# Expert feed-forward in blocks of 32 rows on four column quarters, with two rooms in DRAM for the sums

## The chip, the cores and the metric

The kernel runs on one core of a Trainium2 chip. The metric is device time in microseconds, the median of several executions. TensorE (PE) has a granted clock of 1.2 or 2.4 GHz; VectorE is DVE, ScalarE is ACT, GpSimd is POOL and SyncE is SP, which issues most DMAs.

## What is computed

Eight sequences of 100 tokens (800 in all), width 1024, go through two blocks. Block 0 is a cross attention with 16 heads over 722 context vectors and a mixture of experts; block 1 is another cross attention and a feed-forward with ternary weights. The change touches only the mixture of experts, 32 experts of inner width 512, four for each token:

```python
logits = x @ gate_w.T + gate_b
topk_logits, topk_idx = jax.lax.top_k(logits, K)              # K = 4, E = 32
topk_weight = jax.nn.softmax(topk_logits, axis=-1)
...                                                           # tokens sorted by expert
gate = jax.lax.ragged_dot(xt, w_gate, group_sizes) + b_gate[gid]
up = jax.lax.ragged_dot(xt, w_up, group_sizes) + b_up[gid]
gate = jnp.minimum(gate, 7.0)
up = jnp.clip(up, -7.0, 7.0)
activated = (up + 1.0) * gate * jax.nn.sigmoid(1.702 * gate)
outs = jax.lax.ragged_dot(activated, w_down, group_sizes) + b_down[gid]
...                                                           # back in the tokens' order
y = jnp.sum(outs * topk_weight[..., None], axis=1)
```

Everything is in fp32 here. An fp32 matmul of the program shows as two records in the trace.

## The kernel before

All engines run hand-written streams and meet at semaphores. The expert stage runs from `route_vector` (line 1557) to the sums added to X (lines 1933, 2071).

**Routing.** `route_vector` finds each token's four experts, counts tokens per expert, gives every expert whole blocks of BS rows (64 = P // G with G = 2) and puts a third of the blocks, in a row, on each of NQ_W = 3 queues (`rounds` blocks each): step s works on queue s % 3. An expert that lies across two queues is loaded twice, so there are 34 loads, three of them before the loop. It writes the lists of token indices per tile of 128 rows (`idx`), and the tables `need_b`, `need_d`: how many loads must have landed before step s. `slot_gates` (line 1710) does the gates and the target rows `sidx`, which the steps' columns come from.

**Steps.** `iterations` (line 1867) writes IT = 12 steps out once, and then a loop whose body is again 12 steps, in four guarded rounds of three. In step s the engines do this:

- PE (`moe_tensor`, line 1935; one step from line 1995): wait for weights part A (`m_wga`); first half of gate/up; transposes of the next tile's tokens (`turn`, line 1943, four of the tile's eight) and of the previous step's activations (`turn_act`, line 1959, two); second half of gate/up (part B); the down product of the previous step (line 1975). A block's 64 rows are 64 columns of the array: column half g computes outputs g x 512 to g x 512 + 511 of the gate and up weights, and the two halves work side by side on the same tokens. The down product is split over its 1024 outputs in the same way. So gate/up is 16 matmuls, down 8, each with a moving side of 512.
- DVE (`moe_vector`, line 2039): bias (line 2050), limits, product, into `act`.
- ACT (`moe_scalar`, line 2097): copies the transposes out of PSUM, the sigmoid, and `store` (line 2116): the down result times the row's gate into `ysb`, of which there are two.
- POOL (`moe_pool`, line 1880): gathers each tile's token rows from DRAM (line 1887), and scatters `ysb` with an adding DMA into `acc_d` in DRAM (line 1900), 128 rows of 512 values. Each scatter waits until the one before has landed (`m_sc`), since two blocks may hold the same token. `store` waits for the scatter two steps back.
- SP (`moe_sync`, from line 1780): one round of its loop for each further expert. Its weights come in three parts, A and B (gate/up) and D (down), 2 MB each, into one of three rooms `W2[:, q]`. A and B go out (line 1838) when the last gate/up of the room's former expert is done, the biases when its last `act` is, and D when its last down is.

**The end.** After the last scatter, `m_fin` lets SP load the sums (`yl`, seven tiles, line 1865); DVE adds four to X (line 2071), POOL three (line 1933). In between PE computes the down biases (line 2034). Then the second attention begins; its first loads are in `first_loads` (line 653).

## Time and profile before

| | us |
|---|---|
| median of 3 runs | 3527.59 (3527.23 to 3527.94) |
| the profiled run, its own time | 3528.64 |
| its span | 3526.9 |
| mixture's steps, from DVE's first read of gate/up in step 1 to that in step 68 | 1268.8 to 2041.4 |

The span is the stretch from the first to the last instruction in the profile, and the granted clock is near full throughout. Busy shares are of the whole span. Tables of groups give, for a line and an engine, busy time and mean duration of one, then the idle time of that engine just before these instructions and what ended it. A mean of PE is the duration of a pipelined record, which overlaps its neighbours; the pace is read from starts. In a timeline consecutive instructions of one line are merged.

### The profile page before, as it was taken

What the parts mean: (1) busy time and instruction counts of PE and PEld (TensorE: products, weight loads), DVE (VectorE), ACT (ScalarE), POOL (GpSimd) and SP (SyncE); (2) the same over time, 40 slices, a digit from 0 to 9 for tenths busy, and PEclk for the clock granted to TensorE, in tenths of its full rate; (3) what the DMA queues carried; (4) which work ended last, traced back from release to release, by engine and by line L of the source; (5) the groups of instructions that cost most, each with busy time, mean ns of one, the idle gap of its engine ahead of it and who ended that gap; (6) DMA issues with size and microseconds to landing.
All of it is one profiled execution on the core that took longest, in us unless ns stands there. A gap on an engine that the chain in (4) does not pass through costs nothing.

```text
span 3526.9 us, 43045 instructions
## 1 busy us (share of the span) xinstructions
PE 3433.0 (97%) x16460; PEld 1800.5 (51%) x16461; DVE 1634.7 (46%) x1977; ACT 863.2 (24%) x1256; POOL 746.3 (21%) x709
## 2 busy tenths in 40 slices
PE   7999999999999789999999989999999999999999
PEld 4565565566466333333333346556465564554554
DVE  8764474565466531111111146436355365662661
ACT  2330131032033211111111125335154252220110
POOL 4200400400320012212222220000000002780860
PEclk9999999999999899999999999999999999999999
DMA  7631131132123196899888975436255261430420
GB/s 219 227 101 52 62 88 47 67 100 64 49 69 123 67 376 198 303 380 313 292 294 308 369 240 163 138 126 184 95 166 157 80 163 57 144 142 1 158 93 38
DMA packets 93029, 556.64 MB, mean 158 GB/s; under 512 B 11288, under 2 KB 11424, under 8 KB 74976
## 3 DMA queue, kind: packets, MB, share of 16 engines
q1 hardware_dynamic: 58288, 445.28, 35.5%
q0 software_dynamic: 31392, 93.76, 10.3%
q10 hardware_dynamic: 3216, 15.68, 1.4%
q8 instruction: 101, 1.65, 0.2%
q14 instruction: 32, 0.26, 0.0%
HBM read 517.62 MB, written 40.71 MB: 158 GB/s over the span
## 4 chain that ended last, share of the span: by engine, by line
PE 85%; DMA 6%; DVE 3%; ACT 1%; issue 1%; SPq 0%; POOL 0%; DVEq 0%; POOLq 0%; ACTq 0%
PE PS L964 15%; PE PS L1951 10%; PE PS L2276 10%; PE PS L1111 9%; PE PS L921 8%; PE PS L1975 5%; DMA W<-in_W 5%; PE PS L2302 5%; PE PS L950 4%; PE PS L816 4%; PE PS L833 3%; PE PS L900 2%; PE PS L1047 2%; PE PS L848 2%; PE PS L974 1%; ACT Sb L1250 1%
## 5 line engine op out<-in xcount | busy, mean ns | idle before, releaser
L964 PE MATMUL PS<-Sb,kvN 121*128 121x400 f32 (+1 forms) x1536 | 536.7, 499 | 0.0
L1951 PE MATMUL PS<-W,hT 128*64 128x512 f32 x2208 | 505.1, 599 | 14.8 <-DMA W<-in_W 14.4
L964 PEld LDWEIGHTS PS<-Sb,kvN 121*128 121x128 f32 (+1 forms) x1536 | 286.7, 190 | 205.9 <-issue 2.4
L2276 PE MATMUL PS<-xh,wq 128*128 128x400 f16 x2048 | 348.8, 334 | 1.8 <-DVE xh L1339 1.8
L2050 DVE TENSOR_TENSOR gu<-PS,bias 128x512 f32<-128x512 f32 x69 | 47.7, 691 | 634.4 <-PE PS L1951 607.0
L921 PE MATMUL PS<-kvT,wkr 128*128 128x363 f32 x1024 | 340.4, 475 | 0.0
L1111 PE MATMUL PS<-wb,ctxl 128*128 128x512 f32 x768 | 331.0, 592 | 0.0
L2232 POOL TENSOR_SCALAR gtq<-stg,thr 128x1024 f16<-128x1024 f32 x96 | 289.1, 3026 | 170.2 <-DMA stg<-in_F 142.5
L1951 PEld LDWEIGHTS PS<-W,hT 128*64 128x64 f32 x2208 | 155.5, 138 | 303.4 <-issue 292.8
L1515 POOL TENSOR_TENSOR qrope<-qrope,rt 128x400 f32<-128x400 f32 x156 | 157.5, 1034 | 719.0 <-DVE rt L1377 712.7
L2276 PEld LDWEIGHTS PS<-xh,wq 128*128 128x128 f16 x2048 | 200.8, 98 | 149.2 <-DVE xh L1339 2.3
L1975 PE MATMUL PS<-W,actT 128*64 128x512 f32 x1104 | 250.5, 596 | 2.6 <-ACT actT L2105 2.6
L1111 PEld LDWEIGHTS PS<-wb,ctxl 128*128 128x128 f32 x768 | 145.8, 190 | 181.9 <-issue 179.9
L921 PEld LDWEIGHTS PS<-kvT,wkr 128*128 128x128 f32 x1024 | 185.1, 190 | 100.6 <-issue 2.6
L1422 DVE TENSOR_TENSOR Sb<-Sb,PS 121x2400 f32<-121x2400 f32 x64 | 169.9, 2654 | 91.9 <-PE PS L1033 91.9
L1476 DVE TENSOR_TENSOR X<-PS,X 128x512 f32<-128x512 f32 x96 | 66.3, 691 | 277.0 <-PE PS L1111 277.0
L1163 ACT ACTIVATE KR<-PS 128x726 f32<-128x726 f32 x128 | 99.3, 776 | 375.7 <-PE PS L921 375.7
L816 PE MATMUL PS<-xnT,wq_h 128*128 128x400 f32 x512 | 185.8, 500 | 1.7 <-ACT xnT L515 1.7
L950 PEld LDWEIGHTS PS<-QR,KR 64*121 64x121 f32 x3072 | 168.2, 182 | 33.8 <-issue 32.2
L1438 DVE RECIPROCAL rz<-PS 128x400 f32<-128x400 f32 x64 | 169.5, 2649 | 24.4 <-PE PS L974 24.4
L950 PE MATMUL PS<-QR,KR 64*121 64x100 f32 x3072 | 179.7, 270 | 0.0
L2302 PE MATMUL PS<-wdq,hh 128*128 128x512 f16 x768 | 166.6, 379 | 0.0
(287 smaller groups left out, 3781.3 us busy)
## 6 DMA issues: line engine op xcount, KB each, us to landing
W<-in_W SPq DMA_DIRECT2D x96, 2048.0 KB, 10.7
stg<-in_F SPq DMA_DIRECT2D x32, 1536.0 KB, 6.4
kvT<-kvT_d SPq DMA_DIRECT2D x64, 726.0 KB, 4.3
kvN<-kvN_d SPq DMA_DIRECT2D x64, 726.0 KB
absin<-in_F POOLq DMA_DIRECT2D x48, 512.0 KB, 4.0
hn<-in_F POOLq DMA_DIRECT2D x48, 512.0 KB, 4.7
wb<-in_WB SPq DMA_DIRECT2D x8, 2560.0 KB, 9.5
wc_h<-in_WC SPq DMA_DIRECT2D x32, 576.0 KB, 4.6
```

The costliest lines, as they stand in the source:

```text
L816: mm = nc.tensor.matmul(PS[:, heads_bank(a, half, first), 0:HALF], wq_h[a % 2][:, c * K:(c + 1) * K], xnT[:, c, half * HALF:(half + 1) * H ...
L921: mm = nc.tensor.matmul(PS[:, bank + n, 0:LH], wkr[:, dc, u, w:w + P], kvT[b % 2][:, dc, n * LH:(n + 1) * LH], start=dc == 0, stop=dc == C ...
L950: mm = nc.tensor.matmul(PS[0:LP, score_bank(b, j) + r, to:to + S], KR[b % 2][rows, u, lc * LP:(lc + 1) * LP], QR[rows, q, cols], start=Tru ...
L964: mm = nc.tensor.matmul(PS[:, value_bank(b) + dc, 0:GW], kvN[b % 2][0:k, lc, dc * P:(dc + 1) * P], Sb[b % 2][0:k, lc, :], start=lc == 0, s ...
L1111: mm = nc.tensor.matmul(PS[:, 2 + n % 4, :], ctxl[:, a, m * P:(m + 1) * P], wb[:, w:w + 512], start=a == 0, stop=a == HA - 1)
L1422: nc.vector.tensor_tensor(sb, sb, PS[0:LP, 5, 0:GW].unsqueeze(1).to_broadcast([LP, LC, GW]), ALU.add).then_inc(sem(f"{p}_sb"), 1)
L1438: nc.vector.reciprocal(rz[:, :], PS[:, z_bank(b), 0:GW]).then_inc(sem(f"{p}_rz"), 1)
L1951: mm = nc.tensor.matmul(PS[g * BS:(g + 1) * BS, 2 + u % 2, :], hT2[k][:, c, half * BS:(half + 1) * BS], W2[:, q, o:o + N1], start=c == 0, ...
L1975: mm = nc.tensor.matmul(PS[h * BS:(h + 1) * BS, 4 + u % 2, :], actT[:, j, g * BS:(g + 1) * BS], W2[:, u % NQ_W, o:o + DH], start=c == 0, s ...
L2232: nc.gpsimd.tensor_scalar(gtq[q][:, w, :], stg[q][:, w, :], thr[:, w:w + 1], None, ALU.is_gt).then_inc(sem("f_gt"), 1)
L2276: mm = nc.tensor.matmul(PS[:, 4 * q + 2 * w + half, 0:HALF], wq[q][:, w, c, :], xh[part][:, c, half * HALF:(half + 1) * HALF], start=c == ...
L2302: mm = nc.tensor.matmul(PS[:, n % 8, :], hh[part][:, c, m * P:(m + 1) * P], wdq[:, c, half], start=c == 0 and part == 0, stop=c == EB - 1 ...
```

## The change

G becomes 4: blocks have 32 rows, and four column quarters of the array work side by side, each on a quarter of the outputs, with a moving side of 256 instead of 512. Gate/up is 32 matmuls a step, down 16. A step transposes two of the next tile's eight token chunks and one chunk of activations. A tile of 128 rows now feeds four steps, the written-out body has 24 steps, and the tables are sized for 144 steps; the place arrays are 36 tiles wide instead of 42.

`acc_d` has two rooms, one for even and one for odd steps, each with its semaphore. A scatter waits only for the one two steps back, in the same room, and `ysb` and `gcol` have four rooms (and one for the last step). The last step's scatter goes out alone, after both rooms have ended. At the end both rooms are loaded and added: 14 loads instead of seven, two additions for each tile. The second set of tiles, `yl2`, lies in the space of `kvN` and `wb`, so the loads of these wait until the additions are done. The zero fill of `acc_d` doubles. The tables `need_b` and `need_d` now begin at step 3, with the entries of steps 1 and 2 computed apart (`lead`). Biases come in four DMAs of 32 rows instead of two of 64.

```diff
-G = 2
+G = 4
 BS = P // G
-LB = BS.bit_length() - 1
+LB, LG = BS.bit_length() - 1, G.bit_length() - 1
+NACC = 2
...
-ZROWS = TPAD // HG
-assert ZROWS * HG == TPAD and T + BS <= TPAD
+ZROWS = NACC * TPAD // HG
...
-        acc_d = nc.dram_tensor("acc_d", [G * TPAD, DH], F32, kind="Internal").ap()
+        acc_d = nc.dram_tensor("acc_d", [NACC * G * TPAD, DH], F32, kind="Internal").ap()
...
+        NY = 4
...
+        py6 = Plan(nc, kvn_at, aT_at)
+        yl2 = [py6.put(f"yl2{m}", [P, D]) for m in range(MT)]
...
+                sp.wait_ge(sem("m_bda"), 2 * MT + NACC * 4)
+                sp.wait_ge(sem("m_addp"), NACC * (MT - 4))
...
-            link(dve, ts(bcol[:, :], sq, rounds[:, :], sr, ALU.mult, ALU.add))
-            link(dve, ts(ended[:, :], tend[:, :], bcol[:, :], None, ALU.is_le))
-            vt.tensor_reduce(cols[:, 0:1], ended[:, :], AX, ALU.add).then_inc(sem("m_te"), 1)
+            link(dve, ts(bfirst[:, :], sq, rounds[:, :], None, ALU.mult))
+            link(dve, ts(gone[:, :], tend[:, :], bfirst[:, :], None, ALU.is_le))
+            vt.tensor_reduce(cols[:, 0:1], gone[:, :], AX, ALU.add).then_inc(sem("m_te"), 1)
...
+            for q in range(1, NQ_W):
+                ins = ts(later[0:1, q, :], start[0:1, :], float(q), None, ALU.is_le)
+            link(dve, ins)
+            link(dve, vt.tensor_reduce(lead[0:1, :], later[0:1, 1:NQ_W, :], AX, ALU.add))
+            ts(need_b[0:1, 1:NQ_W], lead[0:1, :], 1.0, float(BI_INC), ALU.add, ALU.mult)
+            ts(need_d[0:1, 1:NQ_W], lead[0:1, :], 1.0, float(DN_INC), ALU.add, ALU.mult)
             dve.wait_ge(sem("m_tet"), 2)
-            ts(need_b[0:1, :], PS[0:1, 1, 0:MAX_STEPS], float(NQ_W - 1), float(BI_INC), ALU.max, ALU.mult)
-            ts(need_d[0:1, :], PS[0:1, 1, 0:MAX_STEPS], float(NQ_W - 1), float(DN_INC), ALU.max, ALU.mult)
+            ts(need_b[0:1, NQ_W:NQ_W + P], PS[0:1, 1, 0:P], float(NQ_W - 1), float(BI_INC), ALU.max, ALU.mult)
+            ts(need_d[0:1, NQ_W:NQ_W + P], PS[0:1, 1, 0:P], float(NQ_W - 1), float(DN_INC), ALU.max, ALU.mult)
...
-                ts(sidx[:, :, h], PS[:, 1, o + MAX_TILES:o + 2 * MAX_TILES], float(G), cst[:, C_HD:C_HD + 1],
+                nc.vector.tensor_copy(Gs[:, 0:MAX_TILES, h], PS[:, 1, o:o + MAX_TILES]).then_inc(sem("m_gs"), 1)
+                ts(sidx[:, :, h], PS[:, 1, o + MAX_TILES:o + 2 * MAX_TILES], float(G), cst[:, C_HD + h % NACC:C_HD + h % NACC + 1],
...
+                for i, room in enumerate((yl, yl2)):
+                    at = i * TPAD + m * P
+                    sp.dma_start(room[m][0:TW[m], :], acc_t[at:at + TW[m], :]).then_inc(sem(f"m_cg{m // 2}"), 16)
...
-                if before:
-                    pool.wait_ge(sem("m_sc"), 16 * s)
+            def scatter(s, room, kc, done):
...
-                                             in_=ysb[k][:, :], in_offset=None, compute_op=ALU.add).then_inc(sem("m_sc"), 16)
+                                             in_=ysb[room][:, :], in_offset=None, compute_op=ALU.add).then_inc(sem(done), 16)
...
+                    for n in range(2):
+                        gate_column(n, n)
+                gate_column(s + 2, (u + 2) % NY)
                 if not (head and u == 0):
-                    scatter(s - 1, (u - 1) % 2, (u - 1) % 2, not (head and u == 1))
+                    k = (u - 1) % NACC
+                    if not (head and u <= NACC):
+                        pool.wait_ge(sem(SC[k]), 8 * s + SC_BASE[k] - 8 * (k + 1))
+                    scatter(s - 1, (u - 1) % NY, k, SC[k])
...
-            gate_column(last, 2)
-            scatter(last, 0, 2, True)
-            pool.wait_ge(sem("m_sc"), 16 * last + 16)
+            ended_at = [pool.value_load(np_i[0:1, 10 + i:11 + i], min_val=8 * (MIN_STEPS - 2), max_val=8 * (MAX_STEPS + 2) + SC_BASE[i]) for i in range(NACC)]
+            gate_column(last, NY)
+            for i in range(NACC):
+                pool.wait_ge(sem(SC[i]), ended_at[i])
             for k in range(2):
                 pool.wait_ge(sem(f"m_hs{k}"), gathered[k])
-            pool.sem_inc(sem("m_fin"), 1)
+            scatter(last, NY, 2, "m_fin")
+            pool.wait_ge(sem("m_fin"), 16)
...
-                nc.gpsimd.tensor_tensor(X[0:TW[m], m, :], yl[m][0:TW[m], :], X[0:TW[m], m, :], ALU.add).then_inc(sem("m_addp"), 1)
+                pool.wait_ge(sem(f"m_cg{m // 2}"), 16 * NACC * min(2, MT - m // 2 * 2))
+                for i, room in enumerate((yl, yl2)):
+                    if i:
+                        pool.wait_ge(sem("m_addp"), NACC * (m - 4) + i)
+                    nc.gpsimd.tensor_tensor(X[0:TW[m], m, :], room[m][0:TW[m], :], X[0:TW[m], m, :], ALU.add).then_inc(sem("m_addp"), 1)
...
-                if not (isinstance(t, int) and t == 0):
-                    pe.wait_ge(sem("m_tpe"), 2 * t - 1 + part)
-                for c in range(4):
-                    cc = 4 * part + c
-                    mm = nc.tensor.transpose(PS[:, 6 + part, c * P:(c + 1) * P], hs[k][:, cc * P:(cc + 1) * P], ident)
+                if not (isinstance(t, int) and t == 0 and part < 2):
+                    pe.wait_ge(sem("m_tpe"), G * t - 1 + part)
+                for c in range(KC // G):
+                    cc = KC // G * part + c
+                    mm = nc.tensor.transpose(PS[:, 6 + part % 2, c * P:(c + 1) * P], hs[k][:, cc * P:(cc + 1) * P], ident)
...
                 for c in cs:
                     for g in range(G):
                         o = c * 2 * FI + g * N1
-                        mm = nc.tensor.matmul(PS[g * BS:(g + 1) * BS, 2 + u % 2, :], hT2[k][:, c, half * BS:(half + 1) * BS],
+                        mm = nc.tensor.matmul(PS[g * BS:(g + 1) * BS, 2 + u % 2, 0:N1], hT2[k][:, c, half * BS:(half + 1) * BS],
                                               W2[:, q, o:o + N1], start=c == 0, stop=c == KC - 1)
...
                     for h in range(G):
                         o = W2_D + c * D + h * DH
-                        mm = nc.tensor.matmul(PS[h * BS:(h + 1) * BS, 4 + u % 2, :], actT[:, j, g * BS:(g + 1) * BS],
+                        mm = nc.tensor.matmul(PS[h * BS:(h + 1) * BS, 4 + u % 2, 0:DH], actT[:, j, g * BS:(g + 1) * BS],
                                               W2[:, u % NQ_W, o:o + DH], start=c == 0, stop=c == IC - 1)
...
-                    nc.vector.tensor_tensor(X[0:TW[m], m, :], yl[m][0:TW[m], :], X[0:TW[m], m, :], ALU.add).then_inc(sem("m_bda"), 1)
-                    dve.wait_ge(sem("m_bda"), 2 * MT + m + 1)
+                    dve.wait_ge(sem(f"m_cg{m // 2}"), 16 * NACC * min(2, MT - m // 2 * 2))
+                    for i, room in enumerate((yl, yl2)):
+                        nc.vector.tensor_tensor(X[0:TW[m], m, :], room[m][0:TW[m], :], X[0:TW[m], m, :], ALU.add).then_inc(sem("m_bda"), 1)
+                        dve.wait_ge(sem("m_bda"), 2 * MT + NACC * m + i + 1)
...
-            def store(s, u, k, kc, columns, scattered):
+            def store(s, u, room, columns):
                 eng.wait_ge(sem("m_gc"), columns)
-                if scattered is not None:
-                    eng.wait_ge(sem("m_sc"), 16 * scattered)
                 eng.wait_ge(sem("m_y"), s + 1)
-                nc.scalar.activation(ysb[k][:, :], PS[:, 4 + u % 2, :], ACT.Copy, scale=gcol[kc][:, 0:1]).then_inc(sem("m_ye"), 1)
+                nc.scalar.activation(ysb[room][:, :], PS[:, 4 + u % 2, 0:DH], ACT.Copy, scale=gcol[room][:, 0:1]).then_inc(sem("m_ye"), 1)
...
+                    k = (u - 1) % NACC
+                    if not (head and u <= NY):
+                        eng.wait_ge(sem(SC[k]), 8 * s + SC_BASE[k] - 8 * (k + 1) - 8 * (NY - NACC))
+                    store(s - 1, (u - 1) % IT, (u - 1) % NY, s)
```

## Rows read from the trace of the kernel before

**Rows 1.** The page's first part: busy time, share, instructions.

```profile
PE 3433.0 (97%) x16460; PEld 1800.5 (51%) x16461; DVE 1634.7 (46%) x1977; ACT 863.2 (24%) x1256; POOL 746.3 (21%) x709
```

**Rows 2.** Groups by line: engine, operation, shape, count, busy, mean ns, idle before.

```profile
L1951 PE MATMUL PS<-W,hT 128*64 128x512 f32 x2208 | 505.1, 599 | 14.8 <-DMA W<-in_W 14.4 <-issue 0.4
...
L1975 PE MATMUL PS<-W,actT 128*64 128x512 f32 x1104 | 250.5, 596 | 2.6 <-ACT actT L2105 2.6
...
L1900 POOL DMA_INDIRECT acc_d<-ysb,sidxc x69 | 109.2, 1582 | 161.7 <-ACT ysb L2116 134.7 <-POOL sidxc L1896 24.3 <-issue 2.7
```

**Rows 3.** Timeline of PE over one step: start us, us, instructions, count.

```profile
1437.22 3.60 PE L1975 MATMUL PS<-W,actT 128*64 128x512 f32 x16
1440.66 3.60 PE L1951 MATMUL PS<-W,hT 128*64 128x512 f32 x16
1444.19 0.65 PE L1943 MATMUL PS<-cst,hs 128*128 128x128 f32 x4
...
1444.99 3.65 PE L1951 MATMUL PS<-W,hT 128*64 128x512 f32 x16
1448.48 1.89 PE L1975 MATMUL PS<-W,actT 128*64 128x512 f32 x8
```

**Rows 4.** Timeline of DVE: its read of gate/up in steps 1 and 68.

```profile
1268.83 0.69 DVE L2050 TENSOR_TENSOR gu<-PS,bias 128x512 f32<-128x512 f32 x1 [5.86 <-PE PS L1951]
...
2041.40 0.69 DVE L2050 TENSOR_TENSOR gu<-PS,bias 128x512 f32<-128x512 f32 x1 [9.12 <-PE PS L1951]
```

**Rows 5.** Groups by line of two other matmuls of the kernel.

```profile
L950 PE MATMUL PS<-QR,KR 64*121 64x100 f32 x3072 | 179.7, 270 | 0.0
...
L1114 PE MATMUL PS<-wb,ctxl 128*32 128x512 f32 x128 | 15.4, 598 | 0.0
```

**Rows 6.** Timeline of PE in the ternary down product.

```profile
3432.92 3.63 PE L2306 MATMUL PS<-wdq,hh 128*32 128x512 f16 x56
3436.49 0.82 PE L2302 MATMUL PS<-wdq,hh 128*128 128x512 f16 x3
```

**Rows 7.** Source line 2004 on PE's sequencer: ns min/median/max, first and last.

```profile
L2004 PEldq TENSOR_LOAD <-need_d x68: 297/302/595, 1259.7 to 2029.2; - x68
```

**Rows 8.** Timeline of SP: issues of experts' part A in two chained stretches.

```profile
1511.80 0.36 SPq L1838 DMA_DIRECT2D W<-in_W  x1
...
1567.66 0.36 SPq L1838 DMA_DIRECT2D W<-in_W  x1
...
1664.79 0.36 SPq L1838 DMA_DIRECT2D W<-in_W  x1
1680.52 0.36 SPq L1838 DMA_DIRECT2D W<-in_W  x1
```

**Rows 9.** Windows: us, PE, PEld, DVE, ACT, POOL busy; clock, DMA share, GB/s.

```profile
1363.00:1372.00 9.00, 9.00 (x46) 3.28 (x44) 1.92 (x5) 1.26 (x3) 1.97 (x3) 1.00 0.22 30
1284.70:1343.10 58.40, 49.67 (x232) 17.76 (x228) 8.19 (x20) 8.66 (x18) 12.16 (x18) 0.94 1.02 383
1336.00:1337.00 1.00, 1.00 (x4) 0.38 (x6) 0.00 (x0) 0.00 (x0) 0.18 (x1) 0.50 0.99 422
```

**Rows 10.** DMA issues from 1284.7 to 1343.1: count, median us to landing.

```profile
acc_d<-ysb,sidxc POOLq DMA_INDIRECT x5, 12.1
```

**Rows 11.** Source line 1900, the adding scatters of the whole stage.

```profile
DMA to landing us min/median/max: 4.5/9.7/14.1
```

**Rows 12.** Timeline of PE after a wait for weights.

```profile
1335.99 5.07 PE L1951 MATMUL PS<-W,hT 128*64 128x512 f32 x16 [6.08 <-DMA W<-in_W]
```

**Rows 13.** Timeline of all engines around the end of the stage.

```profile
2040.08 1.01 POOL L1887 DMA_INDIRECT hs<-h_d,idxc  x1 [0.83 <-POOL idxc L1884]
...
2061.56 3.34 SPq L1865 DMA_DIRECT2D yl<-acc_d  x7
...
2066.39 1.23 DVE L2071 TENSOR_TENSOR X<-yl,X 128x1024 f32<-128x1024 f32 x1 [3.26 <-DMA yl<-acc_d]
...
2072.74 7.93 POOL L1933 TENSOR_TENSOR X<-yl,X 128x1024 f32<-128x1024 f32 x3 [14.32 <-DMA yl<-acc_d]
```

More of the change, by code:

```diff
@@ L323, in build @@
         ended = p3.put("ended", [P, E])
+        bfirst = p3.put("bfirst", [P, 1])
+        lead = p3.put("lead", [P, NQ_W - 1])
+        gone = p3.put("gone", [P, E])
         here = p3.put("here", [P, E])
@@ L1683, in route_vector @@
             vt.tensor_copy(np_i[0:1, 2:3], np_i[0:1, 0:1])
-            link(dve, ts(np_i[0:1, 0:1], np_i[0:1, 0:1], 1, None, ALU.arith_shift_right))
+            ts(np_i[0:1, 8:9], np_i[0:1, 0:1], 1.0, None, ALU.add)
+            vt.tensor_copy(np_i[0:1, 9:10], np_i[0:1, 0:1])
+            link(dve, ts(np_i[0:1, 0:1], np_i[0:1, 0:1], LG, None, ALU.arith_shift_right))
+            link(dve, ts(np_i[0:1, 8:10], np_i[0:1, 8:10], 1, None, ALU.arith_shift_right))
+            for i in range(NACC):
+                ts(np_i[0:1, 10 + i:11 + i], np_i[0:1, 8 + i:9 + i], 16.0, float(SC_BASE[i]), ALU.mult, ALU.add)
             ts(np_i[0:1, 5:6], np_i[0:1, 0:1], 4.0, None, ALU.add)
@@ L2021, in one @@
                     down(s - 1, (u - 1) % IT)
-            for part in range(2):
+            for part in range(G):
                 turn(0, 0, part)
@@ L2098, in turned @@
             def turned(t, k, part):
-                eng.wait_ge(sem("m_tp"), 2 * t + part + 1)
-                nc.scalar.activation(hT2[k][:, 4 * part:4 * part + 4, :].rearrange("p c t -> p (c t)"), PS[:, 6 + part, :],
+                eng.wait_ge(sem("m_tp"), G * t + part + 1)
+                w = KC // G
+                nc.scalar.activation(hT2[k][:, w * part:w * part + w, :].rearrange("p c t -> p (c t)"), PS[:, 6 + part % 2, 0:w * P],
                                      ACT.Copy).then_inc(sem("m_tpe"), 1)
@@ L2132, in moe_scalar @@
             turned_act(last)
-            store(last, NQ_W - 1 + NQ_W, 0, 2, last + 2, last)
+            store(last, NQ_W - 1 + NQ_W, NY, last + 4)
         def down_steps(blk):
```

70 lines of the change are left out of this document (36 added, 34 removed).

## The prediction

> **What bounds the kernel now.** I read the busy line first: TensorE is busy 97% of 3526.9 us, the others 51% and less [rows 1]. A gain must therefore come from PE time, or PE must be made to wait. Then the groups by line: the experts' gate/up and down matmuls (L1951, L1975) are 505.1 + 250.5 = 755.6 us, all with 64 columns of the array and a 512-wide moving side, and in the whole loop they waited only 14.8 us, for weights [rows 2]. Then one step on PE's timeline. A step is three equal pieces of 16 records (first half of gate/up, second half, down of the step before) at 3.44 us from start to start, and 0.80 us of transposes before the next piece: down starts at 1437.22 and again at 1448.48, a step of 11.26 us [rows 3]. VectorE's read of gate/up marks every step: from step 1 at 1268.83 to step 68 at 2041.40 are 67 steps in 772.57 us, 18.2 us more than 67 x 11.26 = 754.4 [rows 4]. So this stage is PE-bound with about 18 us of waits.
>
> How many steps there are follows from the reference: running its router on its inputs gives experts 32, 55, 338, 52, 163, 149, 35, 16, 72, 78, 46, 134, 137, 6, 97, 9, 28, 24, 26, 83, 128, 84, 79, 59, 56, 87, 132, 58, 78, 313, 438 and 108 tokens. In blocks of 64, a third of them in a row on each of three queues taken in turn, that is 67 blocks and 69 steps, as the 69 scatters confirm [rows 2]. In blocks of 32 it is 115 blocks and 117 steps. 48 steps more, each with half the rows.
>
> **1. PE's step.** Each piece has now four quarters side by side with a 256-wide moving side: half as many columns per pass, half the time if four quarters overlap as two halves do. Do they? Two places of this kernel already use 32 columns: L1114, whose 128 records take 15.4 us or 0.120 each, where the 64-column ones of the same width take 505.1/2208 = 0.229 [rows 2, 5], and the ternary down product, 56 records in 3.57 us from start to start, 64 ns each where one quarter alone would take about 215 [rows 6]. So quarters do overlap; a piece takes 3.44/2 = 1.72 us. What stays: the transposes, now three of 128 columns instead of six per step and so 0.3 to 0.45 us, and some 0.15 us of drain: 0.58. To this come register work in PE's sequencer, one table load of 0.30 us and the operations around it per step [rows 7], which the instructions queued ahead cover over 11.26 us and not wholly over half: 0.1 us. Step: 3 x 1.72 + 0.58 + 0.10 = 5.85 us. 68 steps of 11.26 (765.3) become 116 of 5.85 (678.6): **-86.7 us**. Bounds 5.7 and 6.3 us.
>
> One price speaks against it. The shortest matmuls of the trace, 64 columns wide and 100 long, come at 179.7 us / 3072 = 58.5 ns each though at the pace of a step's records (3.44 us for 16 of 512) 100 columns are worth 42 ns [rows 3, 5]; if a pair of load and matmul had such a floor per issue, 96 pairs a step would take 5.6 us + 0.6: 6.2 to 6.3 us. I take the lower value, because the heaviest quarter of the ternary product has 16 of its 56 records, 3.57/16 = 0.223 us each, the pace of 512 columns: it was the columns that set it [rows 6].
>
> The Trainium skill, page "TensorE: Matmul & The Clock Gate", section "Back-to-back issue gap", says that a sustained stream of weight load and matmul pairs is spaced about 81 ns at 128 columns and 131 ns at 512, against columns/2.4 GHz for a matmul alone. By the first figure (an estimate) a step would be 96 x 81 ns + 0.6 = 8.4 us and the kernel near 3800. This trace disagrees: 64 ns per pair of 512 columns in the ternary down product [rows 6].
>
> **2. The loads, which now decide.** An expert's 6.3 MB come in three parts (A, B, D), into the room of the expert that ended last in the same queue. Part A can be issued only when that expert's last gate/up is done; it is needed two other queues' steps and a piece later: before 2 x 11.26 + 3.4 = 25.9 us, after 2 x 5.85 + 1.7 = 13.4 us. Where experts follow each other closely, loads chain and only the DMA engines' rate counts. Chained loads come every 18.6 us (1511.80 to 1567.66 is three) or, once, 15.7 (1664.79 to 1680.52) [rows 8]. In such a stretch the engines are full (share 1.02, 383 GB/s) [rows 9]: nothing is hidden there, it is bandwidth. So the load of an expert pays, per gap of n steps to the next one, 18.6 - n x 5.85 where that is positive.
> From the token list, experts start after at steps 3, 9, 13, 14, 20, 28, 29, 31, 42, 43, 46, 48, 49, 52, 55, 59, 64, 66, 76, 81, 85, 87, 90, 94, 99, 100, 101, 106, 108, 114, 115. Seven gaps of one step (short 12.75 each), five of two (6.9), four of three (1.05): 89.3 + 34.5 + 4.2 = 128 us. They lie in 8 clusters; the first load of each has some 1.5 us in hand (two thirds of 18.6 plus 2 us of latency stay just under the 13.4 + 1.7 at which B is needed): -12. **+116 us**, and the waits of before, 18, are inside that and go: **-18**.
> The same arithmetic on the kernel before (start steps 3, 5, 6, 7, 14, 16, 17, 19, 23, 24, 25, 27, 28, 31, ...; a gap of one is short 7.3, two gain 3.9, about 12 in hand) gives waits at steps 7, 25, 28 and 38 of 11 us together, where the rows give 18. It finds the places and is somewhat low, as it leaves out the crowd behind the head.
>
> **3. Scatters.** There are 117 instead of 69. On GpSimd one is 1.58 us [rows 2]; with copies of its index and gate columns and a quarter of a gather (1.0 us [rows 13]) a step stays under 4 us of 5.85. Landing takes 4.5 / 9.7 / 14.1 us (min, median, max) [rows 11]. With one room each would wait for the last and set a step of 10 us; with two, a room comes round every 11.7 us, and four output rooms on ScalarE's side take up the rest. So the second room is needed, and it hides landings except near 14 us, in full DMA stretches where PE waits for weights anyway. Cost here nil; if that cover is gone, (14.1 - 11.7)/2 = 1.2 us for a step.
> What 128 pieces of 1 KB cost the DMA engines no row shows. The nearest are 2 KB ones: in a window that holds one scatter and no load the share is 0.22 of 9 us, 2.0 us [rows 9]. By bytes the new one costs 1.0, by packet 2.0. By bytes the traffic per time is as before; by packet each of the 16 short gaps is 1.7 us longer, +27. I take bytes, since half as many bytes move per row, and keep both ends.
> Beside loads a scatter landed in 12.1 us [rows 10], against 4.5 at best [rows 11]: they share engines in turn. The skill's page "DMA: Bandwidth & Descriptors", section "Queues, rings and completion order", says that each engine takes turns between queues by packet. With it small pieces would cost a load more than their bytes say; that is the second rival below, and the rows are in line with it.
>
> **4. Clock.** After a wait of 6.08 us the next piece took 5.07 us [rows 12] instead of 3.6 [rows 3], and in the window just after, the granted clock was 0.50, that is 1.2 GHz [rows 9]. After, 10 to 12 waits are that long or longer: 12 x 1.4 = 17, of which half falls while the next load is awaited anyhow. **+7** (0 to 20).
>
> **5. Ends.** From the last gate/up (2041.40 [rows 4]) to the load of the sums (2061.56 [rows 13]) are 20.2 us: last step and scatter. With half a step per stage some 15.5: -4.6. Behind it 14 loads instead of seven (3.34 us of issues, now 6.7), four tiles of 1.2 us added twice on VectorE and three of 2.64 on GpSimd, which has time [rows 13]: the loads' data double, 3.3 MB more at 383 GB/s is 8.6 us, the adds +4.8, together +8 as they overlap. kvN and wb, whose space holds the second room's tiles, are loaded later; first needed well behind that. The zero fill doubles on the scalar queue under the first attention. The routing gains a few one-row operations and loses 14% of the width of its place arrays: +0.5. **+4**.
>
> **6. Code.** The unrolled body is 24 steps instead of 12, so more is fetched: 10 us at most. **+4**.
>
> Sum: -86.7 + 116 - 18 + 7 + 4 + 4 = +26. Against the profiled run's own 3528.64 us (which lies 1.0 above the median 3527.59 and 1.7 above its span): **3555 us**.
>
> **The rivals.**
> A (forecast, 0.50): PE's gain is eaten by the loads; 3535 to 3575.
> B (0.13): loads chain faster than 18.6, since steps and so other traffic pause meanwhile; 15.7 was seen once [rows 8]. At 16.4 us the gaps cost 7 x 10.55 + 5 x 4.7 = 97 less 19 in hand = 78: 3555 - 38 = **3517 us**, faster. Against it: four spacings of 18 to 19.5 against one. It decides below 17 us.
> Between A and B (0.12) it lands within 0.2% (7 us, about what a measurement of this kernel can tell from no change): 3521 to 3535.
> C (0.10): the pair floor of part 1, a step of 6.25 us: 116 x 0.4 = +46, less 0.4 for each of the 7 + 10 + 12 = 29 steps in short gaps, 12: **3589 us**.
> D (0.13): small scatter pieces cost by packet: +27 to 30, and room waits: **3585 us**.
> E (0.02): 81 ns pairs: 3800 us.
> That the change doesn't do what it says would be four quarters not overlapping: a piece of 3.44 us and 117 steps of 11, +500; the rows of part 1 speak against it, and I leave it under 0.01.
>
> **How the numbers follow.** Slower by over 0.2%: A, C, D, E = 0.75. Same 0.12. Faster 0.13. The range from 3520 (B left out) to 3610 (C and D with the upper clock term) holds 0.85.
>
> **What would show it.** Right: 117 scatters; pieces of 32 records 1.72 us apart; steps of 5.8 to 5.9 us in stretches without loads; DMA share near 1 with waits for weights of 11 to 13 us at starts 14, 29, 43, 49, 100, 101, 115, in all 110 to 130 us; part 2 of the page showing a stage of about the same length. Wrong: steps of 6.2 or more (C); loads chained at 16 us (B) or 20 and more (D); PE waiting for ACT's output or GpSimd in steady steps (rooms, part 3); a tail longer than 30 us past the last down.

## The result and the profile after

The changed kernel takes **3627.73 us** (median of four runs, 3624.79 to 3632.71), 1.0289 times the kernel before (95% interval 1.0276 to 1.0302): about 100 us slower, where 27 were forecast and 3610 was the end of the range. The span is 3626.2 us against 3526.9, so +99.3.

The page of the kernel after, its busy line and two groups that answer to [rows 1] and [rows 2]:

```profile
PE 3376.3 (93%) x24321; PEld 1928.9 (53%) x24322; DVE 1667.7 (46%) x2239; ACT 882.8 (24%) x1450; POOL 840.8 (23%) x850
...
L1990 PE MATMUL PS<-W,hT 128*32 128x256 f32 x7488 | 480.7, 400 | 109.5 <-DMA W<-in_W 93.8 <-issue 15.3 <-ACT hT L2141 0.4
...
L1929 POOL DMA_INDIRECT acc_d<-ysb,sidxc x117 | 183.4, 1567 | 407.2 <-ACT ysb L2155 346.9 <-POOL sidxc L1925 27.4 <-issue 18.8
```

PE is busy 57 us less and idle much more, and there are 117 scatters, as forecast. One step on PE's timeline in a calm stretch, the counterpart of [rows 3]:

```profile
1438.62 1.93 PE L1990 MATMUL PS<-W,hT 128*32 128x256 f32 x32
1440.37 1.91 PE L2014 MATMUL PS<-W,actT 128*32 128x256 f32 x32
1442.09 1.91 PE L1990 MATMUL PS<-W,hT 128*32 128x256 f32 x32
1443.93 0.44 PE L1982 MATMUL PS<-cst,hs 128*128 128x128 f32 x2
...
1444.41 1.93 PE L1990 MATMUL PS<-W,hT 128*32 128x256 f32 x32
```

A piece is 1.72 us (1440.37 to 1442.09) and a step 5.79 (1438.62 to 1444.41). So the step is what was worked out for it, and the time is lost between steps. The waits of PE by cause, in the whole kernel after (us, times, longest):

```profile
PE PS L1990 <- DMA W<-in_W: 93.8, 26, 9.0
PE PS L1998 <- issue: 53.8, 1, 53.8
...
PE PS L1990 <- issue: 15.3, 4, 6.8
```

The first row was forecast. The other two were not: PE waits for nothing that the profile names ("issue"), once for 53.8 us and three times for 3 to 7. The 53.8 us lie between the last full step and the last transpose, at the loop's exit. What PE's sequencer did then is seen in its branches: source lines 1904 (the loop) and 1906 (the test of a round) in the kernel after, and the same two lines (1873, 1875) of the kernel before; ns min/median/max, first and last:

```profile
L1906 PEldq COMPARE_BRANCH  x40: 68/71/6644, 1417.6 to 2130.1; - x40
...
L1904 PEldq COMPARE_BRANCH  x5: 86/4687/7837, 1585.8 to 2134.9; - x5
```

```profile
L1875 PEldq COMPARE_BRANCH  x24: 67/68/218, 1392.2 to 2042.3; - x24
...
L1873 PEldq COMPARE_BRANCH  x6: 83/223/237, 1526.5 to 2042.6; - x6
```

Before, the taken branches, five skipped rounds among them, took 0.21 to 0.24 us. After, the taken ones take 3.4 to 7.8 us: three jumps back between iterations, and at the end nine rounds without work and one more jump back, in a row from 2080.7 to 2134.7. Meanwhile a DMA queue that fetches instructions is at work (packets, MB, share of the engines). Its row in the window 2078 to 2140 of after:

```profile
q8 instruction: 20, 0.33, 3.3%
```

Twenty packets of 16 KB for ten jumps, two a jump on average. The same queue over the stretch from step 1 to the last step, in before (1268.8 to 2041.4) and in after (1267.6 to 2080.4):

```profile
q8 instruction: 11, 0.18, 0.1%
```

```profile
q8 instruction: 100, 1.64, 0.8%
```

In before the queue has no packet at all between 1530 and 2040: from its second turn on the loop's body is never fetched again. In after every turn fetches it anew: 20 packets between 1592.6 and 1752.4, besides the two of a jump, for the 5072 instructions that PE and its sequencer show in one iteration. That is 230 to 254 instructions to a packet, an estimate from these counts. So the two traces say which body stayed in place, before any experiment.

Where the 99.3 us lie, by marks in both traces (the reads of gate/up, the first load of the sums, PE's first transpose after it; the marks of before are in [rows 4] and [rows 13]):

| stretch | before | after | difference |
|---|---|---|---|
| start to the read of step 1 | 1268.8 | 1267.6 | -1.2 |
| step 1 to the last step | 772.6 | 812.8 | +40.3 |
| to the first load of the sums | 20.2 | 65.0 | +44.8 |
| to PE's first transpose | 20.0 | 33.3 | +13.3 |
| to the end | 1445.4 | 1447.4 | +2.1 |

The loop stretch of before and of after as windows (columns as in [rows 9]):

```profile
1268.80:2041.40 772.60, 758.21 (x3620) 271.57 (x3618) 137.06 (x335) 130.37 (x268) 173.81 (x268) 0.99 0.86 309
```

```profile
1267.60:2080.40 812.80, 703.08 (x11390) 397.41 (x11385) 159.01 (x575) 150.40 (x460) 256.63 (x401) 0.93 0.80 285
```

PE's busy time there is 758.2 and 703.1 us. Steps at their pace would be 67 x 11.26 = 754.4 and 115 x 5.79 = 665.9; what is over, 3.8 and 37.2, is put down to work at half clock (granted clock 0.99 and 0.93 on average). So the +40.3 are -88.5 of steps, +79.4 of waits for weights (14.4 to 93.8), +33.4 of half clock, +15.3 of jumps back and 0.7 of rest.

### The profile page after: what moved, and what is told of

The parts are those of the page before. It is cut to its first block, busy times and chain, and to the rows that moved or that the text cites. A ratio compares the mean times of both kernels' runs of the same rounds, so it can differ in the third digit from the quotient of the medians.

```text
span 3626.2 us, 60940 instructions
## 1 busy us (share of the span) xinstructions
PE 3376.3 (93%) x24321; PEld 1928.9 (53%) x24322; DVE 1667.7 (46%) x2239; ACT 882.8 (24%) x1450; POOL 840.8 (23%) x850
## 4 chain that ended last, share of the span: by engine, by line
PE 77%; DMA 11%; DVE 4%; issue 2%; ACT 1%; SPq 0%; POOL 0%; DVEq 0%; POOLq 0%; ACTq 0%
PE PS L978 14%; DMA W<-in_W 10%; PE PS L2317 9%; PE PS L1125 9%; PE PS L935 8%; PE PS L1990 7%; PE PS L2343 5%; PE PS L964 4%; PE PS L830 4%; PE PS L2014 3%; PE PS L847 3%; PE PS L914 2%; PE PS L1061 2%; PE PS L862 1%; PE PS L988 1%
## 5 line engine op out<-in xcount | busy, mean ns | idle before, releaser
L1990 PE MATMUL PS<-W,hT 128*32 128x256 f32 x7488 | 480.7, 400 | 109.5 <-DMA W<-in_W 93.8
L1990 PEld LDWEIGHTS PS<-W,hT 128*32 128x32 f32 x7488 | 241.7, 114 | 289.7 <-issue 105.0
L2089 DVE TENSOR_TENSOR gu<-PS,bias 128x256 f32<-128x256 f32 x117 | 49.7, 425 | 645.4 <-PE PS L1990 645.4
L1929 POOL DMA_INDIRECT acc_d<-ysb,sidxc x117 | 183.4, 1567 | 407.2 <-ACT ysb L2155 346.9
L2014 PE MATMUL PS<-W,actT 128*32 128x256 f32 x3744 | 226.5, 382 | 0.6 <-ACT actT L2146 0.4
```

The costliest lines, as they stand in the source:

```text
L1929: nc.gpsimd.indirect_dma_start(out=acc_d[:, :], out_offset=bass.IndirectOffsetOnAxis(ap=sidxc[kc][:, :].bitcast(U32), axis=0), in_=ysb[roo ...
L1990: mm = nc.tensor.matmul(PS[g * BS:(g + 1) * BS, 2 + u % 2, 0:N1], hT2[k][:, c, half * BS:(half + 1) * BS], W2[:, q, o:o + N1], start=c == ...
L2014: mm = nc.tensor.matmul(PS[h * BS:(h + 1) * BS, 4 + u % 2, 0:DH], actT[:, j, g * BS:(g + 1) * BS], W2[:, u % NQ_W, o:o + DH], start=c == 0 ...
```

## Experiments

The theory: two separate costs, bursts of weight loads and jumps to code that has to be fetched. The ratio of each run is to the kernel before, on the same chip. Differences to the kernel after are plain differences of medians from different chips; the kernel before took 1.2 to 2.7 us less there than beside the kernel after, so 3 us of such a difference mean nothing.

**e1_guard**: one test around the loop's body.

```diff
             with eng.Fori(1, MAX_IT) as it:
-                for r in range(RPI):
-                    with eng.If(it * RPI + r < n_r):
+                with eng.If(it * RPI < n_r):
+                    for r in range(RPI):
+                        with eng.If(it * RPI + r < n_r):
```

> The kernel after, with one more test around the whole loop body, so that an iteration with nothing to do is left by one jump instead of eight. Theory (jumps): behind the last step PE's sequencer makes ten taken jumps of 4.6 to 7.8 us, because the 24-step body no longer lies ready beside the engine; nine of them are skipped rounds. Seven of them go: 7 x 4.8 = 34 us less, about 3594 us, and PE's idle time before the last transpose falls from 53.8 to about 20 us. Rival (end of stage): the 53.8 us are a wait that belongs to the end of the stage whatever is skipped (landing of scatters, loads of the next stage); then nothing changes, 3628 us.

Measured: 3591.97 us, ratio 1.0190 (1.0173 to 1.0207), 36 us less than after. PE's waits in it:

```profile
PE PS L1991 <- DMA W<-in_W: 93.9, 26, 8.7
...
PE PS L1991 <- issue: 16.4, 4, 6.9
PE PS L1999 <- issue: 14.1, 1, 14.1
```

Of 53.8 us at the exit 14.1 are left, and neither the loads nor the jumps back changed. The wait at the exit counts skipped rounds. The eighth jump went too: the one that now leaves the last iteration leads over the whole body and is cheap, as the trace of e1_guard says in the window 2095 to 2110:

```profile
L1905 PEldq COMPARE_BRANCH  x1: 240/240/240, 2100.9 to 2100.9; - x1
```

It lands on the code behind the body, from which PE had jumped back 8.5 us earlier. So it isn't the distance that costs. That this code was still in place is the likely reason; no run tests it.

**e4_unroll**: `IT = 6 * G * NQ_W` (72 steps written out, 72 in a body that runs once), and nested rounds:

```diff
+            def rounds_from(it, r):
+                with eng.If(it * RPI + r < n_r):
+                    for u in range(r * NQ_W, (r + 1) * NQ_W):
+                        one(it, u)
+                    if r + 1 < RPI:
+                        rounds_from(it, r + 1)
```

> The kernel after with 72 steps written out ahead of the loop and 72 in its body, which runs once, its rounds nested so that the first one without work jumps to the end. No jump back is left and one skip. Theory (jumps): the three waits behind jumps back (6.8 + 4.6 + 3.3 = 15 us, with about 6 us of half clock behind them) go, and of 53.8 us at the end some 6 stay: -15 - 6 - 48 = -69 us, about 3559 us. Code in a row costs nothing as it is fetched ahead. Rival (fetching in a row costs too): the longer written-out code adds waits of its own in the 72 + 45 steps, over 10 us in all, 3570 us or more. By the end-of-stage rival only the 15 to 21 us go: 3608 us.

Measured: 3570.19 us, ratio 1.0137 (1.0119 to 1.0155), 57.5 us less than after, 11 short of what was expected and on the 3570 us that the rival named. Its waits:

```profile
PE PS L1993 <- DMA W<-in_W: 97.7, 28, 9.0
...
PE PS L2001 <- issue: 4.5, 1, 4.5
```

Of 69.1 us of "issue" 4.5 are left, the one skip. But no wait appears in the long written-out code, so the rival (fetching in a row costs too) falls: code fetched in a row costs no wait here. The 11 us are missing in the loop, whose stretch fell by 9.7 us where 15.3 of idle time went: the loads took 3.9 of it back (a load has time while PE is late, see e10_unroll_half), and PE's busy time (704.1 against 703.1) shows none of the half clock that I had put behind the jumps.

**e3_before_dead**, on the kernel before: eight rounds that are never entered behind the loop.

```diff
+            for r in range(8):
+                with eng.If(n_r < 1):
+                    for u in range((r % RPI) * NQ_W, (r % RPI + 1) * NQ_W):
+                        one(1, u)
```

> The kernel before (64 rows, one room), with eight blocks of three steps added behind its loop that are never entered, so that each costs one taken jump over code that has not been run. Theory (jumps): what costs is the jump to code that must be fetched, in the 64-row kernel too, at about 4.7 us each: 8 x 4.7 = 38, less some 2 us that the queue covers, +36 us, about 3563 us, while the six jumps inside the loop stay at 0.2 us. Rival: the price belongs to the 32-row form or to the crowded DMA engines at that time; then 8 x 0.2 = +2 us, 3529 us.

Measured: 3524.38 us, ratio 1.000 (0.999 to 1.001). It tests nothing: the trace has the same 43045 instructions as before and none of the eight branches, since the condition can be decided when the program is built. It shows only how well two equal programs agree.

**e3b_before_dead**: the same with `n_r < RMIN + 1`, which is known on the chip alone.

> Again the kernel before with eight blocks of three steps behind its loop that are never entered, now under a condition that is only known on the chip (in e3_before_dead the blocks had been removed when the program was built, since their condition could never hold). A block is some 365 instructions of PE, 23 KB, where one of the kernel after is 627, 40 KB. Theory (jumps to code that isn't there cost 4.6 to 5 us each, in any kernel): 8 x 4.7 = 38 us less 2 that are covered, about 3561 us. Rival (distance): a jump of 23 KB lands in what is already fetched ahead and only the longer ones miss: half of that or nothing, 3525 to 3545 us.

Measured: 3554.37 us, ratio 1.0084 (1.0067 to 1.0100), +28. The eight branches, and PE's wait:

```profile
L1879 PEldq COMPARE_BRANCH  x8: 364/3974/7802, 2036.9 to 2067.7; - x8
```

```profile
PE PS L1963 <- issue: 32.8, 1, 32.8
```

So the 64-row kernel pays too, 3.1 to 7.8 us for a jump over some 365 instructions (a quarter of an iteration) of code that isn't there, while its own jumps back and skipped rounds stay at 0.21 to 0.25. The rival (such a short jump is cheap) falls, but for the first of the eight (0.36). With that one cheap and three at 3.1 to 3.2, 28 us came out where 36 were expected.

**e3c_before_body24**: the four dead rounds inside the body of the kernel before.

```diff
+                for r in range(RPI):
+                    with eng.If(n_r < RMIN + 1):
+                        for u in range(r * NQ_W, (r + 1) * NQ_W):
+                            one(it, u)
```

> The kernel before with four blocks of three steps that are never entered inside its loop body, so that the body is 24 steps of code (2900 instructions of PE, 187 KB, where it is 12 steps and 94 KB before, and 24 steps and 321 KB after), with the same work. Theory (the body must fit beside the engine, and 94 KB do while 187 don't): every iteration now has a jump back and four skips at about 4.8 us, 24 us less the 4 us that queued instructions cover, six times: +120 us, about 3645 us, and the jumps back cost over 3 us instead of 0.2. Rival (187 KB still fit or only the jump's length counts): the jumps stay at 0.2 us, +5 us at most.

Measured: 3685.86 us, ratio 1.0451 (1.0434 to 1.0469), +160: the largest effect of this study, from code that is never run. Its branches (dead rounds, jump back) and waits:

```profile
L1879 PEldq COMPARE_BRANCH  x24: 363/5537/8162, 1525.1 to 2200.6; - x24
...
L1873 PEldq COMPARE_BRANCH  x6: 79/4814/8153, 1547.4 to 2205.7; - x6
```

```profile
PE PS L1955 <- issue: 98.2, 5, 27.4
PE PS L1963 <- issue: 62.9, 1, 62.9
```

The same jump back that takes 0.22 us in a body of about 1460 instructions takes 4.6 to 8.2 us in one of about 2900. The size of the body decides, not the rows of a block. It is forty us more than expected, and both places have a share. The four turns of the loop cost 98.2 us rather than 80: the first of each turn's four dead rounds is cheap (0.36 to 0.46), but beside loads the others take 5.0 to 8.2. The exit costs 62.9 rather than 40: the five rounds that the kernel itself skips there, left out of the expectation, now take 3.1 to 5.0 us each, 21 together.

The Trainium skill, page "Runtime: NRT & Kernel Launch", section "Instruction fetch mechanics", gives PE room for 2048 instructions (128 KiB), refilled in blocks of 16 KiB. Of branches it says that a taken one whose target isn't in "the current 2-page window" forces a fetch before execution can go on. The forced fetch agrees with the runs: two packets of 16 KB for a jump, and 230 to 254 instructions to a packet where the page has 256. The window doesn't, if its two pages are these blocks: an iteration of about 1460 instructions, more than five such blocks, jumps back over its whole length in 0.2 us. What would fit the runs is the whole room: bodies of about 2900 (1460 and four dead rounds of 365) and 5070 instructions pay at every jump back. No run lies between 1460 and 2900, so the limit itself isn't measured.

**e5_half_loads**: the loads in the loop bring half of each part, so products use the former expert's values in the other half (the same edit for parts B and D):

```diff
-                sp.dma_start(W2[:, bass.ds(q, 1), 0:W2_A].rearrange("p a n -> p (a n)"), A["W2"][e, :, 0:W2_A]).then_inc(sem("m_wga"), 16)
+                sp.dma_start(W2[:, bass.ds(q, 1), 0:W2_A // 2].rearrange("p a n -> p (a n)"), A["W2"][e, :, 0:W2_A // 2]).then_inc(sem("m_wga"), 16)
...
```

> The kernel after, but the 31 loads inside the loop bring only the first half of each of the three parts of an expert's weights, so part of the products is made with the former expert's values. Theory: the waits for weights (93.8 us) and the half clock behind them (37 us of excess busy time less some 4 that belong to jumps back) go, as a chained load takes 9 us and every window is 13.4: about -125 us, 3503 us, with PE's step unchanged at 5.79 us; the jumps stay. Rival: the step is held up by something that a shorter load doesn't touch (GpSimd's gathers and scatters, the rooms of the sums, a floor per matmul): then waits of other names appear and the gain stays under 90 us, above 3538 us.

Measured: 3511.47 us, ratio 0.9959 (0.9944 to 0.9973), 116 us less than after, 8 short of what was expected. Of 93.8 us of waits for weights these are left; the jumps stay (53.1 us at the exit and 16.0 behind jumps back), and no wait of another name appears in the steps, so the rival falls:

```profile
PE PS L1990 <- DMA W<-in_W: 4.6, 3, 1.9
```

**e10_unroll_half** has both edits:

> Both remedies at once: 72 steps written out, 72 in the body with nested rounds, and half the weights' bytes in the loop's loads (so part of the products uses the former expert's values). If waits for weights and jumps are separate costs they add up: 3627.7 - 57.5 - 116.3 = 3454 us. If one hides in the other (PE idles for the weights while code is fetched) the two together save less, 3470 us or more.

Measured: 3441.01 us, ratio 0.9763 (0.9747 to 0.9779), 187 less than after, 13 more than the sum of both (174). The loop's stretch of e10:

```profile
1266.20:1938.40 672.20, 668.69 (x11393) 384.91 (x11389) 158.79 (x575) 150.26 (x460) 255.94 (x401) 1.00 0.66 200
```

672.2 us for 115 steps, 5.85 each, at full clock. With loads and jumps away nothing else holds the step: neither GpSimd, nor the rooms, nor a floor per matmul. The expectation had the sign of an overlap wrong. Where one cost hides in the other, taking one away alone gains too little and both together gain more than the sum, and so it is here. Taking the jumps out shortens this stretch by 9.7 us with full loads (812.8 to 803.1) and by 23.7 with half loads (695.9 in e5_half_loads to 672.2). One such place shows in the trace of after: the jump back at 1585.8 holds PE for 6.8 us, and the wait for weights at the next step is 5.8 us where others of its kind are 6.9 to 9.0. Loads with their half clock cost 803.1 (this stretch in e4_unroll) - 672.2 = 131 us without jumps, and 812.8 - 695.9 = 117 us beside them.

**e9_quarter_scatter**: a scatter adds 32 of its 128 rows; the rest of the sums is left out.

```diff
-                nc.gpsimd.indirect_dma_start(out=acc_d[:, :], out_offset=bass.IndirectOffsetOnAxis(ap=sidxc[kc][:, :].bitcast(U32), axis=0),
-                                             in_=ysb[room][:, :], in_offset=None, compute_op=ALU.add).then_inc(sem(done), 16)
+                nc.gpsimd.indirect_dma_start(out=acc_d[:, :], out_offset=bass.IndirectOffsetOnAxis(ap=sidxc[kc][0:32, :].bitcast(U32), axis=0),
+                                             in_=ysb[room][0:32, :], in_offset=None, compute_op=ALU.add).then_inc(sem(done), 16)
```

> The kernel after, but each scatter adds only the first 32 of its 128 rows, so three quarters of the experts' outputs are left out. It prices the scatters' share of the DMA engines beside the loads. If a piece of 1 KB costs by its bytes (1.0 us of the 16 engines for a scatter), a chained load of some 18 us becomes 1.6 us shorter, times 16 short gaps: about -25 us, 3603 us. If it costs by packet (2.0 us), twice that: 3578 us. If scatters don't matter to the loads: 3625 us.

Measured: 3606.12 us, ratio 1.0234 (1.0217 to 1.0251), -21.6, of which 18.0 in the loop's stretch (794.8): nearest to the 3603 us of the price by bytes. A window of the kernel after with one scatter and no load says the same, 0.19 x 6 = 1.1 us of the engines against 2.0 for twice the bytes [rows 9]:

```profile
1366.00:1372.00 6.00, 6.00 (x111) 3.48 (x103) 1.37 (x5) 1.33 (x5) 1.88 (x3) 1.00 0.19 22
```

**e7_one_at_a_time**: a scatter waits for the one before it too.

```diff
+                    if not (head and u == 1):
+                        pool.wait_ge(sem(SC[1 - k]), 8 * s + SC_BASE[1 - k] - 8 * (1 - k))
```

> The kernel after, but each scatter waits for the one before it as well as for that of its own room, so only one is under way at a time. The prediction held that a single room would set the step: issue 1.6 us, landing 3.6 to 12.4 (median 10.5) and 0.5 us between. Over 117 steps, with landings of 5 us in the calm and 9 to 10 beside loads, a step is about 9 us: stage 1050 us instead of 813, about 3860 us. Rival (the rooms buy nothing, PE's step stays the bound): 3628 to 3650 us.

Measured: 3720.41 us (two runs only, 3712.11 and 3728.72), ratio 1.0551 (1.0522 to 1.0580), +93, between both. Its waits:

```profile
POOL sidxc L1925 <- DMA acc_d<-ysb,sidxc: 536.8, 109, 12.1
...
ACT ysb L2157 <- DMA acc_d<-ysb,sidxc: 217.3, 42, 12.0
...
PE PS L1984 <- DMA hs<-h_d,idxc: 57.2, 14, 13.0
```

The second room is needed; without it the chain of scatters delays GpSimd's gathers and with them PE. Two more waits of PE that after doesn't have stand before the down product: 20.8 us for ScalarE's `actT` and 30.1 without a name. A step becomes 7.8 us on average (896.6 us for 115), less than the 9 I had taken. A scatter lands in 3.5 / 4.3 / 13.7 us here (min, median, max), and the waits for weights are 41.9 us instead of 93.8.

**e8_tail_one_room**: only the even steps' room is loaded and added at the end (`enumerate((yl,))`), so the odd steps' sums are left out.

> The kernel after, but at the end only the first of the two rooms is loaded and added, so the sums of the odd steps are left out. It prices the second room's part of the tail: by the prediction 8 us, by the trace of after 13 (from the first load of the sums to PE's first transpose 33.3 us against 20.0 before): 3615 us. Rival: the tail is held by something else (clock, the first loads that wait for the adds), then under 4 us.

Measured: 3619.18 us, ratio 1.0264 (1.0247 to 1.0281), -8.5. The tail of after, and then of e8:

```profile
2145.40 7.09 SPq L1896 DMA_DIRECT2D yl<-acc_d  x14
2153.57 2.48 DVE L2111 TENSOR_TENSOR X<-yl,X 128x1024 f32<-128x1024 f32 x2 [1.77 <-DMA yl<-acc_d]
...
2164.41 16.36 POOL L1972 TENSOR_TENSOR X<-yl,X 128x1024 f32<-128x1024 f32 x6 [21.09 <-DMA yl<-acc_d]
2164.70 6.41 DVE L2111 TENSOR_TENSOR X<-yl,X 128x1024 f32<-128x1024 f32 x2
...
2175.67 5.66 DVE L467 TENSOR_SCALAR hn<-X,mv,rstd 128x1024 f32<-128x1024 f32 x2
2178.71 1.94 PE L481 MATMUL PS<-cst,hn 128*128 128x128 f32 x8 [13.59 <-DVE hn L467]
```

```profile
2151.62 3.51 SPq L1896 DMA_DIRECT2D yl<-acc_d  x7
...
2163.35 7.95 POOL L1972 TENSOR_TENSOR X<-yl,X 128x1024 f32<-128x1024 f32 x3 [13.77 <-DMA yl<-acc_d]
...
2173.46 4.48 PE L481 MATMUL PS<-cst,hn 128*128 128x128 f32 x24 [3.60 <-DVE hn L467]
```

From load to transpose 21.8 us instead of 33.3, so up to 11.5 us hang on the second room. Five other runs that load both rooms (e1_guard, e4_unroll, e9_quarter_scatter, e10_unroll_half, e11_early_a) have 29.0 to 29.7 us here, three (after, e5_half_loads, e7_one_at_a_time) 33.2 to 33.4. Against the shorter ones the second room costs 7 to 8 us; why 4 us come and go isn't shown. The whole is 8.5 faster; in the profiled run its loop stretch was 6.7 longer. Such stretches with loads vary by as much between like kernels (812.8 in after, 819.3 in e1_guard, 819.5 here).

**e11_early_a**, on e4_unroll: part A goes out when the first half of the room's last gate/up is done, not the whole.

```diff
-                sp.wait_ge(sem("m_gu"), done)
+                sp.wait_ge(sem("m_ah"), done)
                 sp.dma_start(W2[:, bass.ds(q, 1), 0:W2_A].rearrange("p a n -> p (a n)"), A["W2"][e, :, 0:W2_A]).then_inc(sem("m_wga"), 16)
+                sp.wait_ge(sem("m_gu"), done)
...
-                if cs[-1] == KC - 1:
-                    mm.then_inc(sem("m_gu"), 1)
+                mm.then_inc(sem("m_gu" if cs[-1] == KC - 1 else "m_ah"), 1)
```

> The written-out kernel of e4_unroll, but part A of an expert's weights goes out when the first half of the room's last gate/up is done, 2.3 us earlier (a piece of 1.72 and the transposes). By the theory of bursts each of the eight clusters of close experts begins its chain of loads 2.3 us earlier and ends it so, and the lone waits of 1.4 to 2 us go: about 8 x 2.3 + 3 for the clock = -21 us, 3549 us. Rival (a chain is paced by the landing of the load before, not by the room): nothing, 3570 us.

Measured: 3550.68 us, ratio 1.0077 (1.0060 to 1.0094), -19.5. Waits for weights:

```profile
PE PS L1994 <- DMA W<-in_W: 79.4, 25, 6.9
```

97.7 became 79.4: 18 us, which is eight clusters times 2.3 us of head start. **e12_before_early_a** is the same edit on the kernel before.

> The kernel before with the same earlier issue of part A (4.2 us earlier: a piece of 3.44 and the transposes of 0.8). Before, weights are waited for in few places (14.4 us, and 3.8 of half clock). By the theory of bursts most of these waits are shorter than 4.2 us each or become so: -12 us, about 3514 us. Rival (the waits there are the crowd behind the head, paced by the engines' rate): -4 us or less, 3522 us.

Measured: 3525.76 us, ratio 1.0002 (0.9993 to 1.0011): nothing, and the rival was right.

```profile
PE PS L1952 <- DMA W<-in_W: 15.3, 8, 4.7
```

PE's waits for weights didn't shrink (14.4 to 15.3). On the queue of SyncE 16 of the loads wait for the load before to land, for 100.3 us in before and 106.6 here, so that a room freed earlier doesn't help them. That it is these 16 that PE waits for is argued, not shown. No version here with the whole computation beats the kernel before; the best of the 32-row ones is e11_early_a, 25 us behind it.

## Why the prediction was wrong

The direction, the matmul part and the loads held; one step failed, the one on code, and it is worth most of the 73 us by which 3555 was missed.

- **PE's step.** 5.85 forecast, 5.79 measured. The -86.7 forecast count 116 steps for 68; at the measured pace these are 765.7 - 671.6 = -94. The -88.5 above are for 115 and 67 steps, for which the forecast gives -81.7. Quarters overlap wholly, in fp32 too. Rivals C (floor per pair) and E (81 ns pairs) fall: 32 records in 1.72 us are 54 ns each.
- **Loads and clock.** +116 - 18 + 7 = +105 forecast, 79.4 + 33.4 = +113 measured. The division was off: less waiting, more half clock. I had sized it as half of 12 waits times 1.4 us; it came to 33.4 us more than before. The waits lie at the starts that the list names (14, 29, 43, 49, 100, 101, 115), but take 7.2 to 10.4 us there where 11 to 13 were said. At one start PE can wait twice, for part A and for part B, and the clock then falls twice. On PE's timeline three pieces are long, where a piece is 1.9. Below them is the granted clock in three windows (columns as in [rows 9]):

```profile
1961.63 3.51 PE L1990 MATMUL PS<-W,hT 128*32 128x256 f32 x32 [8.12 <-DMA W<-in_W]
...
1967.53 2.96 PE L1990 MATMUL PS<-W,hT 128*32 128x256 f32 x32 [1.91 <-DMA W<-in_W]
...
1970.18 2.69 PE L2014 MATMUL PS<-W,actT 128*32 128x256 f32 x32
```

```profile
1958.50:1964.50 6.00, 2.87 (x28) 1.38 (x32) 0.00 (x0) 0.00 (x0) 0.00 (x0) 0.50 1.05 408
1965.00:1968.00 3.00, 1.09 (x18) 0.69 (x18) 0.00 (x0) 0.55 (x2) 0.00 (x0) 1.00 1.09 390
1968.50:1971.50 3.00, 3.00 (x33) 1.91 (x29) 0.90 (x4) 0.25 (x1) 0.00 (x0) 0.50 0.78 328
```

  The granted clock is 0.50 (1.2 GHz) under the first piece, 1.00 (2.4 GHz) behind it, and 0.50 again after the second, shorter idle time. That a part of it replaces waiting (a load goes on while PE is slow) is argued, not shown; only the sum of both was priced (117 us beside jumps, 131 without). In the longest burst of after seven issues of part A, the first and the last shown, are 17.8 us apart on average (single ones 14.3 to 21.0), where 18.6 was taken:

```profile
1527.23 0.37 SPq L1867 DMA_DIRECT2D W<-in_W  x1
...
1633.95 0.37 SPq L1867 DMA_DIRECT2D W<-in_W  x1
```

- Rival B (chains under 17 us) and rival D (price by packet, which the prediction calls the second rival in its part 3) both fall; e9_quarter_scatter and the window of one scatter settle D.
- **Scatters.** Costs nil with two rooms, as said: GpSimd and ScalarE never hold PE in steady steps. What a single room would cost was put too high (10 us a step; 7.8 in e7_one_at_a_time).
- **Ends.** To the load of the sums -4.6 was forecast. With the exit's wait nearly gone (e4_unroll) this stretch is 20.4 us with 4.5 of wait in it, so 15.9 where 15.5 was said. Behind it +8 was forecast and +15.4 measured, 13.3 of it to PE's first transpose, of which 7 to 11.5 by the second room (e8_tail_one_room). A tail of over 30 us past the last down, one of the signs of being wrong, came true. The mis-sized term is the overlap of adds and loads. PE's transpose waits for VectorE, not for the end of GpSimd's adds (2180.8, two us after it): the first add starts 8.2 us after the first load's issue instead of 4.8 [rows 13], VectorE's adds with the statistics between them take 17.5 us instead of 9.8, and from there to the transpose are 7.6 instead of 5.4. These are 3.3 + 7.8 + 2.2 us. Four more adds of 1.24 us explain 5 of the 7.8. The rest comes while GpSimd adds beside VectorE: the last two adds of VectorE take 6.4 us together, and `hn` 2.8 us where it was 0.8 in before.
- **Code, the step that failed**: "The unrolled body is 24 steps instead of 12, so more is fetched: 10 us at most. +4". It was priced as a little more streaming. Streaming causes no wait (e4_unroll); what costs is a taken jump to code that isn't in place. The body went from about 1460 instructions (648 matmuls, 648 weight loads and 167 of the sequencer in one iteration) to about 5070, as the quarters double the instructions of a step and the steps double too. Measured: 15.3 us behind jumps back and 53.8 at the exit, 69.1 of idle time, and e4_unroll, which takes all but 4.5 of it away, is 57.5 us faster. The rows of before had held the warning: two kinds of branches, all at 0.07 to 0.24 us, for a body whose size nobody had asked for, and a worst-case loop of which after runs 39 rounds of 48, with nine to skip.

With +62 (57.5 and the 4.5 left in e4_unroll) in place of +4 and +15 in place of +8 the same sum gives 3555 + 58 + 7 = 3620, against 3627.7. The two terms share some 4 us, as the tail of e4_unroll is 29.3 us and not 33.3. In the first term of the prediction 68 x 11.26 is 765.7, not 765.3, which changes nothing.

## What to carry to other kernels

Count the instructions of a loop body on each engine before unrolling it further: with 1460 instructions in the body of PE its jumps took 0.2 us here, with 2900 and more nearly every taken jump took 3 to 8 us, and a worst-case loop with a test per round then pays one for every round it skips; nest the tests so that one jump leaves. Where a step gets shorter, the window in which its data are reloaded shrinks with it: list the steps at which new data begin and sum the shortfall, for an average DMA share of 0.86 says nothing of bursts. Half the work per step is a gain only as far as both of these leave it.

## What was not expected of the hardware

- A jump's price on PE: 0.2 us within a body of about 1460 instructions; 3.0 to 8.3 us when the target had to be fetched. Over all runs it was 4.9 to 8.3 us where the DMA engines' share was over 0.7, and 3.0 to 5.2 us where it was under 0.4.
- Code that is never entered cost 160 us (e3c_before_body24), more than the whole change.
- The other engines never paid: their branches in the same loops took 0.03 to 0.09 us; in one iteration of after VectorE and its sequencer have 354 instructions, the most beside PE's 5072.
- An adding scatter of 128 pieces costs the DMA engines by bytes at this size: 1.1 us for 1 KB pieces, 2.0 for 2 KB.
